# Norm factor and decay as rows through device memory in a chunked gated-delta scan, with block copies on GpSimd

## The reference

```python
h = concat([cls, patches(x) @ W.T + b])                 # 4 x 3137 tokens x 128
n = layernorm(h)
q, k = l2norm(silu(conv4(n @ Wq.T + bq))), l2norm(silu(conv4(n @ Wk.T + bk)))
v = silu(conv4(n @ Wv.T + bv))
alpha, beta = sigmoid(n @ Wa.T + ba), sigmoid(n @ Wb.T + bb)   # one number per token
for t in tokens:                                        # gated delta rule, state S: 128 x 128 per image
    S = alpha[t] * (S - beta[t] * (S @ k[t]) k[t]^T) + beta[t] * v[t] k[t]^T
    o[t] = S @ q[t]
h = h + (zc_rmsnorm(o) * silu(n @ Wg.T + bg)) @ Wo.T + bo
h = h + ffn(layernorm(h))          # weights mixed per image from 8 task vectors; 128 -> 512 -> 128
```

## Time and profile before

| | |
|---|---|
| median of 3 runs | 950.95 us (950.13 to 955.2) |
| the profiled execution's own time | 952.8 us |
| its span, first to last instruction | 951.1 us |
| TensorE busy (matmul) | 866.4 us, 91% |
| VectorE | 672.8 us, 71% |
| ScalarE | 515.1 us, 54% |
| GpSimd | 323.4 us, 34% |
| mean granted TensorE clock | 0.972 |

### The profile page before, as it was taken

The page is one execution under the profiler, slowest core; times in us unless marked ns, Lnnn a source line. Parts: engine busy times, 40 slices in busy tenths (PEclk is TensorE's granted clock), DMA queues, the critical chain, the costliest instruction groups (busy, mean ns, idle before and its releaser), DMA issues. The chain is left out here.

```text
span 951.1 us, 31438 instructions
## 1 busy us (share of the span) xinstructions
PE 866.4 (91%) x11991; PEld 656.8 (69%) x11991; DVE 672.8 (71%) x2445; ACT 515.1 (54%) x1846; POOL 323.4 (34%) x430
## 2 busy tenths in 40 slices
PE   4799999999999999999999999999977699999996
PEld 2467777777777777777776777777666477777675
DVE  4466778777778777777878777777773486777534
ACT  0445555556655565665555565655543346566664
POOL 3112222122222212222222222222210048889875
PEclk9989999999999999999999999999996699999999
DMA  2000111111111000000000000000000214334341
GB/s 53 6 7 7 51 40 51 40 51 46 30 51 41 29 21 26 28 26 29 29 18 29 18 29 26 28 29 13 24 25 12 89 45 122 112 106 128 101 117 56
DMA packets 60160, 42.52 MB, mean 45 GB/s; under 512 B 3233, under 2 KB 52579, under 8 KB 60012
## 3 DMA queue, kind: packets, MB, share of 16 engines
q1 hardware_dynamic: 59163, 39.98, 14.0%
q10 hardware_dynamic: 848, 0.54, 0.2%
HBM read 20.97 MB, written 19.53 MB: 43 GB/s over the span
## 5 line engine op out<-in xcount | busy, mean ns | idle before, releaser
L408 ACT ACTIVATE logit<-bank 128x2 f32<-128x2 f32 x100 | 17.4, 174 | 161.0 <-PE bank L1010 161.0
L1009 PE MATMUL bank<-SA,work 128*128 128x386 f32 x200 | 94.9, 558 | 3.5 <-ACT work L511 2.9
L1500 ACT ACTIVATE work<-bank,b1mix 128x512 f32<-128x512 f32 x96 | 66.0, 687 | 58.2 <-PE bank L1592 58.1
L1618 PEld LDWEIGHTS bank<-work 128*128 128x128 f32 x768 | 89.5, 192 | 11.5 <-issue 11.5
L1618 PE MATMUL bank<-work 128*128 128x128 f32 x768 | 89.6, 275 | 0.0
L1592 PE MATMUL bank<-work 128*128 128x512 f32 x192 | 86.5, 593 | 0.0
L592 POOL TENSOR_TENSOR expo<-euler,logit 128x8 f32<-128x8 f32 x25 | 40.9, 1638 | 133.0 <-ACT logit L408 133.0
L1010 PE MATMUL bank<-SB,work 128*128 128x256 f32 x200 | 61.2, 388 | 0.0
L612 POOL TENSOR_TENSOR oscale<-ovar,half_neg 128x4 f32<-128x4 f32 x25 | 25.2, 1008 | 105.3 <-DVE ovar L854 105.3
L716 DVE TENSOR_TENSOR work<-bank,work 128x128 f32<-128x128 f32 x100 | 29.2, 292 | 44.5 <-PE bank L997 42.7
L1010 PEld LDWEIGHTS bank<-SB,work 128*128 128x128 f32 x200 | 39.5, 197 | 28.6 <-issue 3.1
(11 more groups left out here) (239 smaller groups left out, 2339.9 us busy)
## 6 DMA issues: line engine op xcount, KB each, us to landing
hn_kept<-work SPq DMA_DIRECT2D x25, 256.0 KB, 2.3
hnT_kept<-work SPq DMA_DIRECT2D x25, 256.0 KB, 2.3
work<-hnT_kept SPq DMA_DIRECT2D x25, 256.0 KB, 3.1
work<-hn_kept SPq DMA_DIRECT2D x25, 256.0 KB, 3.3
out_dram<-work SPq DMA_DIRECT2D x24, 256.0 KB, 2.5
tv<-in_L_ffn_tv_W_dram SPq DMA_DIRECT2D x16, 256.0 KB
work<-in_x_dram SPq DMA_DIRECT2D x23, 102.0 KB
work<-in_projections_dram ACTq DMA_DIRECT2D x1, 257.0 KB
```

Source lines behind the costliest of these rows:

```text
L1009: mm(t[:, 0:386], xs[p][:, b, HIST:XW], SA[:, 0:386], start=True, stop=False)
L1500: ins = nc.scalar.activation(hid[f][:, :], ps[:, :], ACT.Relu, bias=b1mix[:, of[0], f:f + 1])
L1618: ins = mm(by4(bank[2 + par])[:, t, :], hid[f][:, t * C:(t + 1) * C], w2T[of[t]][:, f, :], start=(f == 0 and t == 0), stop=(f == FB - 1), ...
```

## The change

The norm factor is no longer spread on GpSimd and transposed 51 wide. One transpose makes 4 rows of 128 from rstd1, ScalarE copies them, SP stores them to device memory and loads them back broadcast over the pixel rows; the row of the ones column stays 1. The decay goes the same way: SP stores the row of decay and glast and loads it back as columns. The six block copies go from ScalarE to GpSimd, the product of level 6 and the og transposes go to bank 7, and several steps move in their queues: wo behind km of the next iteration, xs ahead of the state update, the h0 statistics ahead of new_blocks(3), expo's three operations and kd ahead of new_blocks(4), vt behind it, relu to the end of ScalarE's body, GpSimd's rstd1 ahead of expo.

```diff
-        rmat = tile(NB * KX, NB, KX)
+        rrows = tile(NB * C, NB, C)
-        decay = tile(NB * C, NB, C)
+        decay_g = tile(NB * C + 2 * NB)
+        decay = decay_g[:, 0:NB * C].rearrange("p (b c) -> p b c", b=NB)
+        glast = decay_g[0:1, NB * C:NB * C + 2 * NB]
...
@@ SP
+                if on(j, LE):
+                    s = j + LE
+                    sp.wait_ge(r_row_ready, s + 1)
+                    sp.dma_start(r_dram[s], rrows[64:64 + NB, 0, :]).then_inc(r_out, 16)
+                    sp.wait_ge(r_out, 16 * (s + 1))
...
+                    sp.dma_start(rrows[0:PIX + 1], r_dram[s].partition_broadcast(PIX + 1)).then_inc(rrows_in, 16)
+                    sp.dma_start(rrows[PIX + 2:KX], r_dram[s:s + 1]).then_inc(rrows_in, 16)
                     sp.wait_ge(hnT_ready, s + 1)
                     sp.dma_start(hnT_dram[:, :, bass.ds(s, 1), :].rearrange("b p s c -> p b (s c)"), hnT).then_inc(hnT_out, 16)
+                if on(j, LF):
+                    s = j + LF
+                    sp.wait_ge(glast_ready, s + 1)
+                    sp.dma_start(g_dram[s:s + 1, :], decay_g[0:1, :]).then_inc(g_out, 16)
+                    sp.wait_ge(g_out, 16 * (s + 1))
+                    need(sp, gs_ready, s - 1)
+                    need(sp, state_ready, s - 1)
+                    sp.dma_start(g_raw[s % 2][:, 0:NB], g_dram[s, 0:NB * C].rearrange("(b t) -> t b", b=NB), allow_slow_non_contiguous=True).then_inc(g_in[s % 2], 16)
+                    sp.dma_start(g_raw[s % 2][:, NB:3 * NB], g_dram[s, NB * C:NB * C + 2 * NB].partition_broadcast(D)).then_inc(g_in[s % 2], 16)
@@ ScalarE
                     nc.scalar.activation(qT[p], by4(bank[4]), ACT.Silu).then_inc(qT_ready, 1)
+                    act.wait_ge(r_row_ps, s + 1)
+                    nc.scalar.copy(rrows[64:64 + NB, 0, :], bank[7][0:NB, 0:C]).then_inc(r_row_ready, 1)
...
-                    act.wait_ge(Y_ready, 5 * (s + 1))
-                    for r in (0, 1):
-                        nc.scalar.copy(Y[sub(r), :, sub(r)], Yd[par][sub(r)])
-                    for r in (2, 3, 0, 1):
-                        nc.scalar.copy(X[par][sub(r), :, sub(r)], Xd[par][sub(r)])
...
@@ ScalarE: behind the level-5 copies and cdecay now stand the shifted xs, level 6, ogT, and relu last
@@ GpSimd
-                    nc.gpsimd.tensor_copy(rmat[:, :, 0:PIX + 1], rstd1[:, :].unsqueeze(2).broadcast_to([D, NB, PIX + 1])).then_inc(rmat_ready, 1)
-                    nc.gpsimd.tensor_copy(rmat[:, :, PIX + 2:KX], rstd1[:, :].unsqueeze(2)).then_inc(rmat_ready, 1)
+                if on(j, LI):
+                    pool.wait_ge(Y_ready, 5 * (s + 1))
+                    for r in (0, 1):
+                        ins = nc.gpsimd.tensor_copy(Y[sub(r), :, sub(r)], Yd[par][sub(r)])
+                    ins.then_inc(Yd_kept, 1)
+                    for r in (2, 3, 0, 1):
+                        ins = nc.gpsimd.tensor_copy(X[par][sub(r), :, sub(r)], Xd[par][sub(r)])
+                    ins.then_inc(Xd_kept, 1)
@@ VectorE
-                    dve.wait_ge(g_ps, s + 1)
-                    nc.vector.tensor_copy(gs[par][:, 4:12], small_ps[:, 20:28]).then_inc(alpha0_kept, 1)
-                    nc.vector.tensor_tensor(gs[par][:, 0:4], small_ps[:, 16:20], gs[par][:, 8:12], ALU.mult).then_inc(gs_ready, 1)
+                    dve.wait_ge(g_in[par], 32 * (s // 2 + 1))
+                    nc.vector.tensor_tensor(gs[par][:, :], g_raw[par][:, 0:NB], g_raw[par][:, 2 * NB:3 * NB], ALU.mult).then_inc(gs_ready, 1)
...
@@ VectorE, between cneg and the state update
+                if on(j, LE):
+                    s = j + LE
+                    dve.wait_ge(rrows_in, 32 * (s + 1))
...
+                    nc.vector.tensor_tensor(xs[par][0:KX, :, HIST:XW], rrows[0:KX], xt[par][0:KX, :, :],
+                                            ALU.mult).then_inc(xs_ready, 1)
@@ TensorE, level 6
-                        pe.wait_ge(X5_ready, s0 + 1)
+                        pe.wait_ge(Yd_kept, s0 + 1)
+                        pe.wait_ge(Y5_ready, s0 + 1)
...
-                            ins = mm(by64(blk_ps)[64:128, b], Bm[par][0:64, b, 64:128], Y[0:64, b, :], start=True, stop=True)
+                            ins = mm(by64(bank[7])[64:128, b], Bm[par][0:64, b, 64:128], Y[0:64, b, :], start=True, stop=True)
@@ TensorE, behind the q product
+                if E_:
+                    pe.wait_ge(rstd1_ready, e + 1)
+                    need(pe, ogT_ready, c)
+                    tr(bank[7][0:NB, 0:C], rstd1[:, :], ident[:, :]).then_inc(r_row_ps, 1)
@@ TensorE, behind km (before: at the end of the body, with C_ and c)
+                if H_:
+                    pe.wait_ge(ogT_ready, h + 1)
...
+                        ins = mm(by4(bank[6])[:, b, :], ogT[:, b, :], Wo_T[:, :], start=True, stop=True)
```

More of the change, by code:

```diff
@@ L175, in vit_tower @@
         qn2e = [sb(f"qn2e{i}", [D, NB]) for i in range(2)]
-        glast = sb("glast", [1, 2 * NB])
-        gs = [sb(f"gs{i}", [D, 12]) for i in range(2)]
+        gs = [sb(f"gs{i}", [D, NB]) for i in range(2)]
+        g_raw = [sb(f"g_raw{i}", [D, 3 * NB]) for i in range(2)]
         so2 = sb("so2", [D, NB])
@@ L242, in vit_tower @@
         rstd1_ready = sem("rstd1_ready")
[L243 to L244 removed]
+        r_out = sem("r_out")
+        r_row_ps = sem("r_row_ps")
+        r_row_ready = sem("r_row_ready")
+        rrows_set = sem("rrows_set")
+        rrows_in = sem("rrows_in")
         hist_ready = sem("hist_ready")
@@ L769, in body @@
                 grow(2)
[L770 to L796, removed]
-                                                      ALU.subtract, ALU.mult)
-                    ins.then_inc(hn_ready, 1)
-                grow(3)
                 if on(j, LE):
@@ L816, in body @@
                     ins.then_inc(mv1_ready, 1)
-                new_blocks(4)
+                new_blocks(3)
+                if on(j, LH):
+                    s = j + LH
+                    h = h1buf[:, :, bass.ds(s, 1), :].rearrange("p b s c -> p b (s c)")
+                    dve.wait_ge(mv2_ready, s + 1)
+                    dve.wait_ge(rstd2_ready, s + 1)
+                    need(dve, hnT_ps, s)
+                    need(dve, hn_out, 16 * s)
+                    for b in range(NB):
+                        ins = nc.vector.tensor_scalar(hn[:, b, :], h[:, b, :], mv2[:, b, 0:1], rstd2[:, b:b + 1],
+                                                      ALU.subtract, ALU.mult)
+                    ins.then_inc(hn_ready, 1)
+                grow(3)
                 if on(j, LF):
@@ L1017, in body @@
                     ins.then_inc(km_ps, 1)
+                if H_:
+                    pe.wait_ge(ogT_ready, h + 1)
+                    need(pe, hnT_ready, h)
+                    need(pe, o_ready, h + 1)
+                    for b in range(NB):
+                        ins = mm(by4(bank[6])[:, b, :], ogT[:, b, :], Wo_T[:, :], start=True, stop=True)
+                    ins.then_inc(wo_ps, 1)
                 level_blocks(1)
```

165 lines of the change are left out of this document (87 added, 78 removed).

## The result

The changed kernel takes **892.33 us** (median of 4 runs, 891.43 to 895.05) against 951.12 for the kernel before in the same session (4 runs, 950.13 to 955.2): a ratio of 0.9379, 95% interval 0.9344 to 0.9414, or 58.8 us less. The forecast was 897, with 889 to 922 as its range. The profiled execution took 895.05, its span 893.2; against the span before, 951.1, it is 57.9 less, and that difference is what is accounted for here. The times given are medians of each kernel's runs, and runs more than 1.5% above the fastest of the same kernel, which only the kernel with the late row has, are not compared.

What follows compares the result with a forecast made beforehand. The scan was taken as bound by TensorE's instructions plus 1.62 us waiting per chunk, VectorE taking over by 0.12. Waits 38.3 plus work 24.0, less 2.5 and 4, made 56; 952.8 - 56 = 897 us, range 889 to 922.

Steps and rivals of the forecast that it cites:

- TensorE waiting at level 1 blocks for Yd: Sign on TensorE, at the next chunk's level-1 blocks, that was to show the prediction wrong altogether; no size given.
- Its own loop: VectorE from TensorE's level 5 to Yd, then TensorE's level 1 to 5: 25.07 us per chunk, against TensorE's 24.95.
- 27.53 - 1.06 - 0.56: TensorE's chunk before, less its waits at level 6 and the norm-factor transposes; with -1.10 + 0.14 it gives 24.95 us.
- The wait at L976 goes because six block copies leave ScalarE: TensorE's wait at level 6, 1.06 us per chunk: ScalarE's level-5 copies end 1.8 earlier, so it disappears.
- new_blocks(4): VectorE's level-4 step, behind kd and expo's wait: ends about 414.0, in time for TensorE with 0.1 us to spare.
- The row chain: Norm-factor row through ScalarE's copy, SP's write and loads: lands 0.7 us before VectorE's xs wants it, so hidden.
- Rival (a): The norm-factor row lands 0.9 us late for VectorE's xs: 20 us in all, 917 us; chance 0.20.
- The decay chain: Decay row written and gathered back by SP, landing at 425.1: hidden by 3.7 us before it delays TensorE.
- Rival (c): The decay gather of 512 single elements takes 11.2 us, 3.7 late: 980 us, slower than before; chance 0.07.
- The port: SBUF port shared by VectorE and GpSimd: GpSimd's pow doesn't hold up VectorE's xs, cost zero.
- Rival (b): GpSimd's pow holds VectorE's xs 0.5 us per chunk: 11 us in all, 908 us; chance 0.06.
- 4 for the first two and last three chunks: Deduction of 4 us at the scan's edges, for row-chain exposures and gain swallowed by other waits in a half-empty pipeline.

Runs made afterwards that it cites:

- e6: The changed kernel with one more 128x128 VectorE copy per chunk, behind qn2e and ahead of the N6 copy: 894.84 us, ratio 0.9391.
- e7: The changed kernel with one more 128x4 transpose per chunk on TensorE, ahead of level 6: 891.99 us, ratio 0.9362.
- e11: The changed kernel with xs on GpSimd and VectorE's state update moved ahead of glast, ovar, kn and cneg: 879.87 us, ratio 0.9248.
- e8: The changed kernel with the xs product on GpSimd, behind the six copies and ahead of oscale: 879.86 us, ratio 0.9226.
- e1: The kernel before with only the six block copies moved from ScalarE to GpSimd: 923.82 us, ratio 0.9695.
- e2: The changed kernel with the six copies back on ScalarE, level 6 still not waiting for X5: 898.39 us, ratio 0.9418.
- e9: The changed kernel with the six copies back on ScalarE and level 6 waiting for X5 again: 910.5 us, ratio 0.9573.
- e10: The changed kernel with two more round trips through device memory for the norm-factor row: one run 936.34 us, three 950.98 to 955.27.
- e5: The changed kernel with SyncE waiting for the row loads, a marker write behind them, and for the decay gathers: one run, 895.22 us.
- e3: The changed kernel with the decay brought to columns by TensorE again, without its transfers: 899.99 us, ratio 0.9434.

## Why the prediction was right, and where it was off

**The chunk.** Forecast 25.07, measured 25.17, and set by VectorE, as forecast and as e6 and e7 show. VectorE's stretch from TensorE's level 5 to the end of Yd is 8.96 (413.23 to 422.19) where the prediction had 8.86, TensorE's part of the loop 16.07 against 16.10, and the hand-over at the end 0.14 against 0.10 for both. The prediction contradicted itself here: it gave "TensorE waiting at level 1 blocks for Yd" as a sign of being wrong altogether, and just this wait appeared, 0.20 in a full chunk. Its own loop, longer than TensorE's work by 0.12, implies such a wait; the sum was right and the sign was wrong.

**TensorE's own time** was mis-sized: forecast 24.95, measured 24.69. The step that failed is "27.53 - 1.06 - 0.56". Those brackets count idle time from a modelled end of the matmul before. Two more lines of the kernel before's timeline of TensorE, which stand ahead of the two waits of the earlier trace rows:

```profile
419.23 1.06 PE L1106 MATMUL bank<-work 128*128 128x128 f32 x8
...
423.59 0.66 PE L1119 MATMUL bank<-ident,work 128*128 128x128 f32 x4
```

By distances of starts, L1106 to L976 was 2.12 (421.35 - 419.23), and the same pair, L1159 to L1016, is 0.98 now, so 1.14 went; L1119 to L1132 was 1.22 (424.81 - 423.59), where the same transposes need 0.49 when nothing holds them (510.50 to 510.99 in e11), so 0.73 went. The waits removed were 1.87 and not 1.62. The new transpose cost 0.20 instead of 0.14. That makes 24.76, and 0.07 stay open. Since VectorE sets the chunk, this had no effect on the time; it does set what e8 could gain.

**"The wait at L976 goes because six block copies leave ScalarE"** was right for that edit alone (e1) but not the whole reason. The diff also drops X5 from level 6's wait, which the prediction's working left out. e2 and e9 separate the two: 12 us for the wait, 6 at most for the copies behind it.

**GpSimd.** Six copies at 0.60 for two and 1.27 for four are 1.87 against 1.8, hidden as forecast, and oscale isn't late. new_blocks(4) held: L744 ends at 410.71 and its update L1038 starts at 410.93, straight behind the work before it.

**The row chain** was right in its verdict and off in its links. From the row's copy to xs the prediction had 6.01 us, and there are 6.16 (410.33 to 416.49). The write took 1.2 to 2.0 instead of 2.3, the loads 2.1 to 3.4 from the first issue instead of 3.04. The forecast margin of 0.7 is the worst case of what was found, 0.75 to 2.8. Rival (a) did not come to pass. Its mechanism is right: in e10 an xs that waits 1.91 for the row makes TensorE wait 1.94. Its price leaves out the loss of clock that stood behind such waits in e10.

**The decay chain** hides. In e5 its loads are in some 3 us before gs asks for them; the forecast had 2.3 there (427.4 - 425.1), and the other 1.4 of its 3.7 behind gs, which no run tests. Rival (c) fell by e5. What the decay's detour gives is 6 to 8 us (e3), less than its 0.56 times 21, because VectorE takes over.

**The port.** Zero for the pow was right: xs took 0.68, over which the pow ran from 416.03 to 417.03. The pow starts first, and xs takes the same 0.68 in all 25 chunks. Rival (b) fell.

**The sum.** The prediction had 51.7 in the full chunks and 4.1 in the edges and nothing in the FFN; measured were 49.1, 9.8 and -1.0. The term "4 for the first two and last three chunks", an estimate of exposures in the half-empty pipeline, was wrong: the edges gained more than their share. The errors have opposite signs, 2.6 us too much in the chunks and 5.7 too little at the edges, and leave 56 against 57.9 in the profiled executions. That the total came so near is in part luck. The other 2.7 between 897 and 892.3 is what the profiled execution took above the median. In the edges no wait was traced to its cause.

## What to carry to other kernels

When an edit both moves work out of a queue and relaxes the wait at its end, each alone may remove the same stall: list every changed wait before pricing the moves, and undo them one at a time. Read idle time on a pipelined engine from the distance of successive starts against the same pair without a wait, and look for small waits that the view of waits doesn't list. A chain through device memory is cheap on the engine that it relieves, but its margin should be counted with the slowest landing seen, since a late one costs the wait and may cost TensorE's clock behind it.

## What the runs showed of the hardware

- **A wait may cost twice.** TensorE's 1.94 idle in e10 was followed by 4.7 us at a mean granted clock of 0.64, and its 2.18 in the chunk before by 5 us at 0.52. The 2.30 at 128.51 in the same trace was followed by 1.00 and km matmuls of 1.06, and so were the waits of 1.08 in e9. What decides between the two stays open.
- **Small transfers.** A write of 2 KB was confirmed 1.17 to 1.96 behind its issue in the changed kernel, most often 1.2, and 2.36 once in e11, against a median of 2.3 for 256 KB; 98 KB broadcast to 49 partitions and one row more landed in 1.8 to 3.1 behind the second issue; 512 single elements of 4 bytes in 2.1 in the median. The 17,100 more packets under 512 B (3,233 to 20,357 on the page) left no wait that the views show.
- **The port shared by VectorE and GpSimd.** A four-element copy from SBUF to SBUF ended with GpSimd's product, 0.5 late (e8), and so did a four-element product of two SBUF tiles, 1.1 late (e11); a product of two SBUF tensors did not wait for GpSimd's pow (0.68 in the changed kernel), nor did an operation with one PSUM input wait for GpSimd's product (1.10 in e11).
